# Summing the weighted V rows in PSUM by plain products with the identity instead of transposing sums, with three residual buffers and an earlier place for one copy of row numbers

## The reference, cut to what matters

```
z = layernorm(x) * g1 + b1
q, k, v = z @ Wq + bq, z @ Wk + bk, z @ Wv + bv          # 8 heads of 64
scores = sum_d(q[row] * k[col]) / 8 + edge_bias            # per edge and head
p = exp(scores - segment_max(scores, row)[row])
out = segment_sum(p / segment_sum(p, row)[row] * v[col], row)
x = x + out @ Wo + bo
x = x + silu(layernorm2(x) @ W1 + b1) @ W2 + b2            # 512 -> 1024 -> 512
return layernorm(previous x + this x)
```

## Time and profile before

| | us |
|---|---|
| median of 3 runs | 3471.95 |
| the runs | 3471.95, 3470.25, 13540.88 |
| the profiled execution | 3467.36 |
| its span, first to last instruction | 3465.6 |
| PE busy | 2801.8 (81%) |
| DVE busy | 2586.1 (75%) |
| POOL busy | 2363.3 (68%) |
| ACT busy | 1732.6 (50%) |

### The profile page before, as it was taken

One profiled execution on the slowest core, in us unless ns is written; L12 is line 12 of the kernel. 1 busy time (PEld: TensorE's weight loads), 2 busy tenths in 40 slices (PEclk: granted clock), 3 DMA queues, 4 the chain that ended last, 5 costly groups with the idle time before them and its releaser, 6 DMA issues.

```text
span 3465.6 us, 82992 instructions
## 1 busy us (share of the span) xinstructions
PE 2801.8 (81%) x18957; PEld 2153.2 (62%) x18958; DVE 2586.1 (75%) x6243; ACT 1732.6 (50%) x6760; POOL 2363.3 (68%) x2599
## 2 busy tenths in 40 slices
PE   8666666666666666477999999999999999999997
PEld 7433333333333333266888888888888888787885
DVE  9877667766766776467787888888877777777774
ACT  0111111111111111157787888888877777787774
POOL 0477777777777777677777777776666666666661
PEclk9866776666667776689999999999999999999999
DMA  8222222222232222378798888888788888888770
GB/s 303 84 80 79 79 81 80 90 82 77 78 81 81 77 77 79 119 279 320 296 335 308 320 312 324 317 315 317 280 304 286 319 286 320 290 294 308 253 266 25
DMA packets 287972, 719.26 MB, mean 208 GB/s; under 512 B 89203, under 2 KB 105779, under 8 KB 287686
## 3 DMA queue, kind: packets, MB, share of 16 engines
q0 software_dynamic: 214080, 585.55, 47.8%
q1 hardware_dynamic: 73862, 133.41, 11.8%
HBM read 725.41 MB, written 72.97 MB: 230 GB/s over the span
## 4 chain that ended last, share of the span: by engine, by line
issue 30%; POOL 27%; PE 16%; DMA 10%; ACT 7%; POOLq 4%; DVE 3%; ACTq 2%; DVEq 0%; SPq 0%; PEld 0%; PEldq 0%
POOL records L413 19%; POOL region_a L537 8%; ACT region_c L740 6%; DMA records<-region_c,pos_i 6%; PE bank L1474 6%; PE wide L1533 2%; PE bank L1374 2%; PE wide L1545 2%; DMA region_c<-x_rows,row_x 2%; PE wide L1492 2%; PE bank L1517 1%; ACTq L740 1%; ACTq L778 1%; DVE region_c L978 1%; PE wide L1502 1%
## 5 line engine op out<-in xcount | busy, mean ns | idle before, releaser
L537 POOL DMA_INDIRECT region_a<-kv,cols x1176 | 1172.4, 997 | 428.1 <-issue 409.5
L413 POOL DMA_INDIRECT records<-region_c,pos_i x1024 | 1010.6, 987 | 444.6 <-issue 410.8
L740 ACT ACTIVATE region_c<-region_a,pr 128x64 f32 x4704 | 1171.1, 336 | 0.0
L1034 DVE TENSOR_TENSOR region_c<-region_a,bank 128x1024 f32<-128x1024 f32 x588 | 681.1, 1214 | 60.8 <-SPq L371 47.2
L1474 PE MATMUL bank<-ident,region_c 128*128 128x128 f32 x4704 | 595.9, 281 | 95.0 <-DVE region_c L1034 94.8
L1474 PEld LDWEIGHTS bank<-ident,region_c 128*128 128x128 f32 x4704 | 569.1, 195 | 125.7 <-issue 111.4
L1492 PE MATMUL wide<-ident,region_c 128*128 128x128 f32 x4704 | 576.5, 276 | 25.9 <-ACT region_c L740 14.0
L1492 PEld LDWEIGHTS wide<-ident,region_c 128*128 128x128 f32 x4704 | 523.4, 144 | 67.4 <-ACT region_c L740 67.4
L660 ACT COPY region_c<-region_a 128x64 f32 x128 | 32.5, 254 | 1062.5 <-DMA records<-region_c,pos_i 1062.5
L1432 PE MATMUL bank<-region_b,region_a 128*128 128x512 f32 x768 | 491.2, 798 | 0.0
L1432 PEld LDWEIGHTS bank<-region_b,region_a 128*128 128x128 f32 x768 | 189.7, 260 | 253.7 <-issue 253.7
(11 more groups left out here) (197 smaller groups left out, 3276.4 us busy)
## 6 DMA issues: line engine op xcount, KB each, us to landing
region_a<-srcT SPq DMA_DIRECT2D x128, 256.0 KB
region_a<-kv,cols POOLq DMA_INDIRECT x1176
region_a<-hiT SPq DMA_DIRECT2D x256, 64.0 KB
records<-region_c,pos_i POOLq DMA_INDIRECT x1024
x_rows<-region_c SPq DMA_DIRECT2D x32, 512.0 KB
kv<-region_a SPq DMA_DIRECT2D x32, 512.0 KB
records<-region_c SPq DMA_DIRECT2D x32, 480.0 KB, 15.0
region_a<-in_x_dram SPq DMA_DIRECT2D x32, 256.0 KB
```

Source lines behind the costliest of these rows:

```text
L413: pool.indirect_dma_start(records, bass.IndirectOffsetOnAxis(ap=pos_i[j % 2][:, s:s + 1], axis=0), rec_w[j % 2][:, s, :], None).then_inc(S ...
L537: pool.indirect_dma_start(KV[r][:, s, :], None, kv, bass.IndirectOffsetOnAxis(ap=cols[r][:, s:s + 1], axis=0), bounds_check=L - 1, oob_is_ ...
L740: last = act.activation(vw[:, s, of], v_part[:, s, C + hd * D:C + (hd + 1) * D], ACT.Copy, scale=pr[:, s + 1, hd:hd + 1])
L1034: last = dve.tensor_tensor(prods[:, of, :], kv_in[:, of, 0:C], q_ps[:, :].unsqueeze(1).broadcast_to([P, 2, C]), ALU.mult)
```

## The change: what it does

- `sum_v` becomes 8 plain products to a block, one for each slot: the identity is the stationary operand and a slot's 512 columns of `vw` the moving one, and all add straight to `acc_ps`, the right way round. `vT_ps`, `vT_sb`, `take_vT`, `turn_sum` and their semaphores go.
- Pair 0 of `sum_v` waits for `acc_taken`, which DVE's `scale` (or, in stage 1, its taking of the finished sum) raises in the same block. `scale` waits for `summed3`, the end of `sum_v` in the block before.
- The sums of the scores are transposing sums before and after.
- `s_all` holds three tiles (`KEPT = 3`), so that DVE waits for an output sent one tile earlier than before. POOL waits for the sent output before it overwrites `out_idx`.
- POOL's wait for the row load of x and the copy to `row_x` move from the start of the tile to its pass `i == 1`, behind the sending of the output.

```diff
+KEPT = 3
-        s_all, z2 = part(2 * C), part(C)
+        s_all, z2 = part(KEPT * C), part(C)
-        scT_sb, vT_sb = part(2 * P), part(C)
+        scT_sb = part(2 * P)
-        vT_ps, acc_ps = bank[1], bank[7]
+        acc_ps = bank[7]
...
 # POOL, tail_rows (pass i == 1)
                 with pool.If(t > 3):
                     sent_tile = pool.snap(nc.s_assert_within(t - 4, 0, NT - 5, skip_runtime_bounds_check_because="the If has t > 3"))
+                    with pool.If(t > 4):
+                        hold(S["out_sent"], pool.snap(n_sent) * 16)
                     take_rows(out_idx[:, :], tile_row(bass.ds(sent_tile, 1))[:, 0:1])
...
+                with pool.If(t > 0):
+                    hold(S["xb_loaded"], pool.snap(n_x) * 16)
+                    copy_rows(row_x[:, :], ...)
 # POOL, row_numbers (start of the tile)
-                with pool.If(t > 0):
-                    hold(S["xb_loaded"], pool.snap(n_x) * 16)
-                    copy_rows(row_x[:, :], ...)
...
 # ACT
-            def take_vT():
-
-                act.wait_ge(SUMMED[3], now)
-                act.wait_ge(S["acc_ready"], groups)
-                act.copy(vT_sb, vT_ps[:, :]).then_inc(S["vT_sb_ready"], 1)
...
 # DVE
             def scale():
 
-                dve.wait_ge(S["acc_ready"], groups)
+                dve.wait_ge(SUMMED[3], groups)
...
-                        with dve.If(t > 3):
+                        with dve.If(t > 4):
                             dve.reg_add(sent, sent, 16)
                             hold(S["out_sent"], dve.snap(sent))
-                        residual(summed(q_at))
+                        residual(summed(s_here))
...
 # PE
-            def sum_v(pair):
+            def sum_v(pair, first=False):
 
                 if pair == 0:
-                    pe.wait_ge(S["vT_sb_ready"], groups)
+                    pe.wait_ge(S["acc_taken"], now)
                 pe.wait_ge(V_READY[pair], ahead)
                 for s in (2 * pair, 2 * pair + 1):
-                    for c in range(KT):
-                        last = pe.matmul(vT_ps[:, c * P:(c + 1) * P], vw[:, s, c * P:(c + 1) * P], ident[:, :],
-                                         start=s == 0 and c == 0, stop=s == GROUP - 1, is_transpose=True,
-                                         skip_group_check=True)
+                    last = pe.matmul(acc_ps, ident[:, :], vw[:, s, :], start=first and s == 0, stop=s == GROUP - 1,
+                                     skip_group_check=True)
                 last.then_inc(SUMMED[pair], 1)
-
-            def turn_sum(first=False):
-
-                pe.wait_ge(S["vT_sb_ready"], groups)
-                pe.wait_ge(S["acc_taken"], groups)
-                for c in range(KT):
-                    last = pe.matmul(acc_ps[:, c * P:(c + 1) * P], vT_sb[:, c * P:(c + 1) * P], ident[:, :],
-                                     start=first and c == 0, stop=c == KT - 1, is_transpose=True, skip_group_check=True)
-                last.then_inc(S["acc_ready"], 1)
...
                 sum_d(0)
-                if stage < 2:
-                    with pe.If(t > 0):
-                        turn_sum()
-                else:
-                    turn_sum(stage == 2)
                 sum_d(1)
```

More of the change, by code:

```diff
@@ L425, in _ @@
             pool.wait_ge(S["rows_ready"], 1)
-            names = "groups now ring side off page_left late pages since n_resets n_late n_row n_sent n_x count ahead left".split()
-            groups, now, ring, side, off, page_left, late, pages, since, n_resets, n_late, n_row, n_sent, n_x, count, ahead, left = (
+            names = "groups now ring side off page_left late pages since n_resets n_late n_row n_sent n_x count ahead left kept".split()
+            groups, now, ring, side, off, page_left, late, pages, since, n_resets, n_late, n_row, n_sent, n_x, count, ahead, left, kept = (
                 pool.alloc_register(f"pool_{name}") for name in names)
-            for r in (groups, ring, side, off, late, pages, since, n_resets, n_late, n_row, n_sent, n_x, ahead):
+            for r in (groups, ring, side, off, late, pages, since, n_resets, n_late, n_row, n_sent, n_x, ahead, kept):
                 pool.reg_mov(r, 0)
@@ L547, in tail_rows @@
                     hold(S["out_ready"], pool.snap(n_sent))
-                    with pool.If(pool.snap(side) > 0):
-                        send(1)
+                    with pool.If(pool.snap(kept) < 1):
+                        send(0)
+                        pool.reg_mov(kept, 1)
                     with pool.Else():
-                        send(0)
+                        with pool.If(pool.snap(kept) < 2):
+                            send(1)
+                            pool.reg_mov(kept, 2)
+                        with pool.Else():
+                            send(2)
+                            pool.reg_mov(kept, 0)
+                with pool.If(t > 0):
+                    hold(S["xb_loaded"], pool.snap(n_x) * 16)
+                    copy_rows(row_x[:, :], tile_row(bass.ds(pool.snap(nc.s_assert_within(t - 1, 0, NT - 2, skip_runtime_bounds_check_because="the If has t > 0")), 1))[:, 0:1])
                 pool.nop()
@@ L725, in exponents, with weigh @@
                 act.copy(sc[:, 0, :], m_run[:, :]).then_inc(S["max_kept"], 1)
-            def weigh(pair, reg, freed, t=None, first=False):
+            def weigh(pair, reg, freed):
                 v_part = region_a[:, bass.ds(act.snap(reg, min_val=0, max_val=(RING - 1) * HALF), HALF)].rearrange("p (s c) -> p s c", s=GROUP)
@@ L731, in weigh @@
                 for s in (2 * pair, 2 * pair + 1):
[L732 to L735, removed]
-                        else:
-                            take_vT()
                     for hd in range(HEADS):
@@ L779, in body @@
                 exponents()
-                weigh(0, at, now, t, i is None)
+                weigh(0, at, now)
                 if i is None:
@@ L1006, in _ @@
             dve.wait_ge(S["qkv_out"], 32 * NT)
-            groups, now, at, was, off, front, page_left, late, count, coming, q_at, other_at, front_now, older, oldest, sent, bias_at = (dve.alloc_register(f"dve_{n}") for n in (
-                "groups", "now", "at", "was", "off", "front", "page_left", "late", "count", "coming", "q_at", "other_at", "front_now", "older", "oldest", "sent", "bias_at"))
+            groups, now, at, was, off, front, page_left, late, count, coming, q_at, s_here, s_prior, front_now, older, oldest, sent, bias_at = (dve.alloc_register(f"dve_{n}") for n in (
+                "groups", "now", "at", "was", "off", "front", "page_left", "late", "count", "coming", "q_at", "s_here", "s_prior", "front_now", "older", "oldest", "sent", "bias_at"))
             for r in (groups, at, was, off, front, late, q_at, older, oldest, sent):
@@ L1011, in _ @@
             dve.reg_mov(now, 1)
-            dve.reg_mov(other_at, C)
+            dve.reg_mov(s_here, C)
+            dve.reg_mov(s_prior, 0)
             dve.memset(mv[:, :], 1.0)
@@ L1221, in body @@
                             dve.reg_add(oldest, oldest, 1)
-                            there = summed(other_at)
+                            there = summed(s_prior)
                             dve.wait_ge(S["y_done"], dve.snap(dve.snap(oldest) + 1))
@@ L1291, in body @@
                     dve.reg_mov(late, 0)
[L1292 to L1293 removed]
+                    dve.reg_mov(q_at, dve.snap(dve.snap(q_at) * -1 + C))
+                    dve.reg_mov(s_prior, s_here)
+                    dve.reg_mov(s_here, dve.snap(dve.snap(dve.snap(s_here) + C) % (KEPT * C)))
                     with dve.If(t > 0):
@@ L1461, in _ @@
             pe.reg_mov(ahead, RING)
-            for sem_of in ("y_taken", "y_done", "z2_turned", "acc_ready", "summed0", "summed1", "summed2", "summed3"):
+            for sem_of in ("y_taken", "y_done", "z2_turned", "summed0", "summed1", "summed2", "summed3"):
                 pe.sem_inc(S[sem_of], 1)
@@ L1588, in body @@
                 else:
-                    sum_v(0)
+                    sum_v(0, stage == 1)
                     sum_v(1)
```

26 lines of the change are left out of this document (11 added, 15 removed).

## The result

| | before | after |
|---|---|---|
| median | 3472.18 us (4 runs) | 3780.27 us (4 runs, 3778.18 to 3782.12) |
| profiled execution | 3467.36 us | 3778.18 us |
| its span | 3465.6 us | 3776.4 us |

The ratio is 1.0889, with a 95% interval of 1.0868 to 1.0911. One run of the kernel before, of 13540.88 us, was disturbed and is in no ratio. The forecast was 3824 us in a range of 3770 to 3900: the way and most of the size were right, and 44 us of the forecast rise weren't there.

The account below looks back on a forecast made before the run. The prediction took PE, busy 95% of the second phase, as the bound, with POOL a near second. 3467.4 us + 417.5 for the sum of V - 60.9 of closed waits = 3824 us, range 3770 to 3900.

Parts of the forecast that it names:

- The price of the sum: PE's `sum_v`: 8 plain products cost 6.87 us, less 3.59 and 0.44 removed: +2.84 us a block, +417.5 us.
- Rival 1: `sum_v` on PE: 16 records at 0.117 us each, so POOL becomes the bound, about 3370 us; 3%.
- Waits that the view shows: PE's waits: 14.0 us for ACT's last pair and 46.9 us for DVE's products go, together -60.9 us.
- waits for products: PE waiting for DVE's products: all 46.9 us go, since POOL and DVE get 2.84 us more a block.
- waits that close on PE: PE: 14.0 us of `sum_v` waiting for ACT's last pair and 46.9 us for products go, -60.9 us.
- DVE's scaling: DVE's 95.5 us wait for `turn_sum` ends; PE's new wait on `scale` has 1.6 us slack at its tightest; cost 0.
- the residual buffers: Three buffers remove DVE's 59.7 us of waiting for the sent output; nothing more on PE's path.
- the row numbers: POOL's later wait and copy remove 57.6 us of standing ahead of a tile's gathers; worth 0.
- Rival 3: PE's new wait on DVE's `scale` binds: 3971 us if 1 us in every block, 3856 if in stage 0 alone; 13%.
- Rival 2: POOL sets the pace and PE has hidden slack: 2.84 us would hide, time within 2% of before; 2%.
- Rival 4: PE's waits stay or more close: 3871 us with the 46.9 kept, 3798 with the 25.9 gone too; within forecast's spread.
- the one behind the copy of the scores: PE's 25.9 us of waiting behind ACT's copy of the scores stay, as nothing is put into that gap.

Follow-up runs that it names:

- `sum_only`: The kernel before with V summed by plain products alone, keeping two residual buffers and the early row numbers: 3782.57 us, ratio 1.0898.

## Why the prediction was right, and where it was off

**What bounds the kernel: right.** PE, against the chain of waits, which named POOL. Cutting the products into narrower ones moved the time as PE's load moves (40 us measured, 37 from the records), leaving out half of them took 387 of 506 us, and `sum_only` shows POOL's 60 us of standing still at no cost once PE has more to do.

**The price of the sum: near, and the last digits are luck.** +2.84 us a block and +417.5 us were forecast, +417.1 measured. Two misses of 12 us cancel in that. The plain sum costs 6.95 us a block and not 6.87, in all 1021.9 and not 1009.9, since the first record of a block takes longer. The transposing sum and its turn stand in the kernel before with 604.8 us and not with 147 x (3.59 + 0.44) = 592.4. With pair 3 made short on ACT they take 522.3 + 69.4 = 591.7, so about 13 us of the 604.8 were waiting for pair 3 and not the price of the products. The products alone cost some 430 us more, and 13 us of hidden waiting closed. The row of the same form was the right one to take; the rule on the spacing of loads and products in the Trainium skill, page "TensorE: Matmul & The Clock Gate", section "Back-to-back issue gap", doesn't hold here for float32: records of 512 columns run 0.43 us, against its 0.13. Rival 1 is refuted in its condition: its records would have had to take 0.25 us or less.

**Waits that the view shows: -60.9 forecast, -55.1 measured.** The waits for products kept 3.8 us, and the new wait for `scale` cost 2.6, once, in the tail.

**The mis-sized term.** This is the step that the prediction got wrong: its "waits that close on PE" took ACT's pair 3 at the 14.0 us that PE's view of waits gives. The same wait, seen from PE's loading of stationary operands in the kernel before (PEld, from 1500 us on: total, times, longest), is much larger:

```profile
PEld wide L1492 <- ACT region_c L740: 67.4, 146, 0.8
```

146 times, so in every block. In 120 of them the small piece stood just ahead, and since the end of a product's record is modelled (0.60 us for two records that take 0.43), the record covers the gap and the wait counts as busy time. Of the 67.4 us the view of PE's waits has 14.0; the 34.6 of the feed-forward part and the 13 of the sum account for most of the rest. It could have been read from the timeline alone: 0.70 us between 2563.57 and 2564.27 for two half-wide records, where 0.43 is their pace.

A misread row stood in the way. The earlier trace rows and the prediction take its 3.93 us as the weighing of pairs 3 and 0, and give pair 3 the first half. But 16 instructions of 64 columns are two slots of 8 heads, one pair: the 3.93 us are pair 3 alone. Pair 0 comes behind the exponents, in two groups of 8. The first is:

```profile
2034.25 2.02 ACT L740 ACTIVATE region_c<-region_a,pr 128x64 f32 x8
```

Read as a half, pair 3 would have been ready 1.8 us after the start of `turn_scores`. In truth its weighing begins 0.16 us before that start and ends 3.77 us behind it, where the transposing sum wanted the pair at 0.47 + 2.66 + 0.43 = 3.56. The change wants it 2.6 us later, and the hidden waits close with the 14.0 us. That the 14.0 us go was forecast rightly, but by a comparison with the wrong figure, and the prediction did not ask whether they were all.

**Slower stretches: missed, 11 us.** `sum_d` became 11.0 us cheaper without a change of its own. About half of that lies between 1500 and 1700 us, where PE had often stood: a record of `sum_d` took 0.125 us on average in the kernel before and 0.114 after, at a granted clock of 0.96 before and 1.00 after (1.00 is the level of 2.4 GHz, 0.5 that of 1.2). The prediction has no term for it.

**DVE's scaling, the residual buffers and the row numbers: right at 0** on PE's path (`sum_only` against the changed kernel, 2 us, within the noise). Rival 3 didn't come about. Rival 2, that 2.84 us would hide, is refuted. Rival 4's direction, that more waits close, is what happened, though not its place: the one behind the copy of the scores stayed, at 25.4 us.

## What to carry to other kernels

Price a product by its records and its columns, from a row of the same type: one record for a transposing product in float32, two for a plain one, so here a transposing sum was the cheaper way to add float32 tiles, and a second cheap turn paid for itself. Where `vw` may be rounded to float32r, the plain sum is cheaper than both (8 x 0.245 = 2.0 us a block against 4.0). Read waits on PE in both of its views, products and loads, and check a group's distance between starts against its known pace; a wait that ends within the modelled tail of a record is booked as work. Count the instructions of a row before you say what it covers. And when a sum meets its forecast to a microsecond, compare its two sides one by one. An edit that only closes waits has no value of its own: the same two edits were worth 35 us where several engines were nearly equally busy, and nothing clear of noise where PE was plainly the bound.

## What the runs showed of the hardware beyond that

- A product of 512 columns with both operands in float32r is one record of 0.245 us, against 2 x 0.43 us in float32.
- Waits on PE can cost twice. In the kernel before with pair 3 weighed early, 24 transposing records behind a wait of 1.88 us took 4.10 us (2512.72 to 2516.82) and not 2.66. The granted clock was 1.00 until 2513 and 0.50 from 2514 to 2517. From 1500 to 3400 us it was 0.97 in that run and 0.99 in the kernel before; in the float32r kernel with the same move it was 0.92.
